# Four graph layers on one core: node numbers kept in SBUF, node phase 2 from centred rows

## The chip, the cores and the metric

One core of a Trainium2 chip runs the kernel. The metric is device time in microseconds, the median of several executions. The profile is of one execution. The engines are TensorE (PE), VectorE (DVE), ScalarE (ACT), GpSimd (POOL) and SyncE (SP), which here only issues and orders DMAs. Operands live in SBUF, with 128 partitions; PSUM takes the results of TensorE.

## The reference

Inputs are x with 64 features per node, src and dst (200,000 edges, dst sorted) and edge attributes. Four layers follow one another, each a residual and a layer norm:

```python
def _layernorm(x): ...                      # over the 64 features
x = _layernorm(x + L0(x, src, dst))         # 4-head attention q.k, gate, norm, PReLU
x = _layernorm(x + L1(x, edge_attr_64))     # graph attention over x[src] + bond, 2 heads
x = _layernorm(x + L2(x, edge_attr_64, ...))# edge attention with messages from [x[src], eh]
x = _layernorm(x + L3(x, edge_attr_32))     # two-layer messages, mean over a node's edges
# L3, for each of its two message layers l:
h = relu(concatenate([x[src], edge_attr]) @ msg_w1[l] + msg_b1[l])
msg += h @ msg_w2[l] + msg_b2[l]
```

Every layer gathers rows by src (one row of a table per edge), computes something per edge, and sums over the edges of each dst, with a running softmax in layers 0 to 2.

## The kernel before

**Layout.** The edges lie in order over the 128 partitions, 1568 per partition (`edges_pp`), 56 chunks of J = 28 edges per partition. Two chunks, b = 0 and b = 1, make a round: 28 rounds for each layer. Nodes lie 98 per partition, in 15 groups for the node phases (up to G = 7 each). A prologue builds tables and masks; then an edge phase and a node phase alternate, k = 0 to 3.

**An edge phase** (class `EdgePhase`) has one program on each engine.

- GpSimd (`gpsimd`, L958 to L984) makes the rows of a chunk: for each of the 28 columns one indirect DMA (L982) gathers 128 table rows, one per partition, by a column of node numbers. Before a chunk it waits for the index tile (`index_in[b]`) and for the chunk's rows to be free (`rows_free[b]`, given by the engine that read the previous contents last). It skips the last column of a chunk b = 1 (`by_sync`) and, every second round, in phases 0, 1 and 3, the one before it (`by_scalar`). The last two columns have semaphores of their own, `last_in` and `other_in`, in the opening rounds in which GpSimd gathers them itself.
- SyncE (`sync`, L781, its `turn`) makes, for each chunk: a wait for each of the seven parts of the gathers of chunk b (so that the index tile may be overwritten), the load of the index tile for the next round (L787, 14 KB), the load of the edge attributes (L791) after `attr_free`, 64 single-row fetches (L871, `fetch`) by numbers that it reads into registers, and, after `ready`, the store of the chunk's sums (L794). Once a round it places the 128 fetched rows as one column of the chunk b = 1 (`place`, L879 to L886). The loop holds two rounds, so that its jump falls between two rounds every second time.
- ScalarE does the exponentials (L1087) and copies, and in phases 0, 1 and 3 fetches 128 rows in two rounds, 32 per chunk (`fetch_rows`, also L871), laid as a column by `lay_rows`.
- VectorE does scans and products. In phase 0 it multiplies k by q (L1355), waits for ScalarE's exponentials, multiplies v by the weights (L1363), which frees the rows, and scans the sums (L1367).
- TensorE works in phases 2 and 3. Phase 2 makes messages and keys for groups of QUAD = 4 columns. Phase 3 multiplies the edge attributes into `e_banks` (L1932, seven 512-wide products for each chunk), which VectorE adds to the gathered hidden rows (L1982); ScalarE applies Relu (L1940), which frees the rows. Semaphore `added` lets TensorE overwrite the banks.

**Node phase 2** (`node_phase_2`, L2581 to L2731) works through the 15 groups in stages written as `in_turn(groups, (delay, stage), ..., per=4)`: on each engine, group g's stage comes at a place that its delay sets. GpSimd gathers the summed rows of the nodes (98 gathers). Aggregation, product with W_out, residual, norm, affine, second norm; then x is scaled by 1 / standard deviation on ScalarE (`finish`, one ACTIVATE per row of 64, L2136), turned and multiplied by the hidden weights on TensorE (L2634); VectorE adds b1 (`take_hidden`, L2718) and SyncE stores the group to `hidden_table`, from which phase 3 gathers. For the first 12 groups a second product of x goes to `aux`. `Norm.turn_over` leaves the reciprocal root in `ph.var`.

Of the kernel before, what the change touches and what calls it, by code (L numbers as in the profile page):

```python
# [29 lines left out]
P = 128  # L30
J = 28
G = 7
# [40 lines left out]
class Program:  # L73


    def __init__(self, nc, ins, out, n_nodes, real_pp, ctx):
# [49 lines left out]
        self.first_src = keep("first_src", [P, 3 * J], U32)  # L126
# [6 lines left out]
        self.skip_gate = keep("skip_gate", [P, self.nodes_pp])  # L133
        self.msg_bias = keep("msg_bias", [P, FD])
# [186 lines left out]
def search_phase(p, sems):  # L321
# [8 lines left out]
    with ExitStack() as ctx:  # L330
# [46 lines left out]
        def _(e):  # L377
# [7 lines left out]
            load(e, p.first_src[:, :], ins["src"][:, 0:3 * J])  # L385
# [44 lines left out]
        def _(e):  # L430
# [9 lines left out]
            for n in range(p.begun):  # L440
                e.indirect_dma_start(p.qv_tiles[n // J][:, n % J, :], None, p.qv_table,
                                     bass.IndirectOffsetOnAxis(ap=p.first_src[:, n:n + 1], axis=0))\
                    .then_inc(p.qv_gathered[n // J][n % J // QUAD], 16)
# [252 lines left out]
class EdgePhase:  # L696


    def __init__(self, p, layer, ctx, gather_from, gather_into, parts=1, gathered=None, merged=False):
# [16 lines left out]
        self.index = [self.sb(f"ix{b}", [P, J], U32) for b in (0, 1)]  # L716
        self.index_in = [self.sem(f"index_in{b}") for b in (0, 1)]
# [63 lines left out]
    def sync(self, e, attrs, size=J):  # L781
# [4 lines left out]
        def load_index(b, now):  # L786
            e.dma_start(self.index[b][:, :], p.ins["src"][:, now]).then_inc(self.index_in[b], 16)  # L787

# [11 lines left out]
        def turn(i, helped=False, helps_next=False, others=None):  # L800
            if helped:
                self.place(e, i, helps_next)
            for b in (0, 1):
                for c in range(self.parts):
                    self.wait_part(e, i, b, c, placed=False)
                if b and self.sync_helps and not helped:
                    self.tell_last(e, i + 1)
                if b and others is not None:
                    hold(e, self.other_in, others, self.passed)
                load_index(b, bass.ds(i * (2 * J) + (2 + b) * J, J))  # L810
# [147 lines left out]
    def gpsimd(self, e):  # L958
# [3 lines left out]
        for i in range(self.rounds):  # L962
            for b in (0, 1):
                n = 2 * i + b
                u = self.buffer(i, b)[0]
                now = self.index[b][:, :] if n >= len(self.gathered) else self.p.first_src[:, n * J:(n + 1) * J]
                if n >= len(self.gathered):
                    e.wait_ge(self.index_in[b], 16 * i)
                    if self.begun and n in (3, 4):
                        e.wait_ge(self.rows_free[1 - b], 2)  # L970
                    else:
                        e.wait_ge(self.rows_free[b], i + 1)
                last = self.p.last if n == self.p.chunks - 1 else J
                for j in range(last):
# [3 lines left out]
                    if J * n + j < done or (last_alone and self.by_sync(i)) or (other_alone and self.by_scalar(i)):  # L978
                        continue
                    landed = self.last_in if last_alone else self.other_in if other_alone else \  # L980
# [13 lines left out]
    def wait_part(self, e, i, b, c, placed=True):  # L994
# [11 lines left out]
        if not self.begun:  # L1006
            e.wait_ge(self.gathered[u][c], at(i, columns - off * b, columns - off * b))
        elif isinstance(i, int) and i < 2:
            e.wait_ge(self.gathered[u][c], (columns, columns - off, columns, 2 * columns - off)[2 * i + b])
        else:  # L1010
            more = columns if b else -off
            if placed:
                e.wait_ge(self.gathered[u][c], at(i, columns - off * b, more))
            else:
                hold(e, self.gathered[u][c - 1], at(i, columns, columns * b), self.passed)
                hold(e, self.gathered[u][c], at(i, columns - off * b, more), self.passed)
        if b and placed and self.sync_helps:
            e.wait_ge(self.placed, at(i, 16, 16))
        if b and placed and self.scalar_step:
# [624 lines left out]
def edge_phase_2(p):  # L1644
# [5 lines left out]
    with ExitStack() as ctx:  # L1650
# [9 lines left out]
        product = ph.sb("product", [P, J, FD])  # L1660
# [149 lines left out]
        def _(e):  # L1810
# [21 lines left out]
            def weigh(i, b, c):  # L1832
# [4 lines left out]
                e.tensor_tensor(product[:, now, :], mk_ps[u][:, :, FD:], q_now[u][:, :, :], ALU.mult)  # L1837
# [3 lines left out]
                e.tensor_reduce(score[:, 0, now], product[:, now, :], AX.X, ALU.add)  # L1841
# [46 lines left out]
def edge_phase_3(p):  # L1888
# [4 lines left out]
    with ExitStack() as ctx:  # L1893
# [32 lines left out]
        def _(e):  # L1926
            with e.Fori(0, ph.rounds) as i:
                for b in (0, 1):
                    ph.wait_attrs(e, i, b, 1)
                    e.wait_ge(added, at(i, 2, b + 1))  # L1930
                    for q in range(quads):
                        last = e.matmul(e_banks[:, q, :], ea_t[b][:, q, :], p.w3_e, start=True, stop=True)  # L1932
# [36 lines left out]
        def _(e):  # L1969
            e.sem_inc(added, 1)  # L1970
            ph.clear_carries(e)
            e.memset(mask[:, :, 0], 0.0)

# [607 lines left out]
def node_phase_2(p):  # L2581
# [3 lines left out]
    with ExitStack() as ctx:  # L2585
# [39 lines left out]
        def _(e):  # L2625
# [3 lines left out]
            def multiply_next(g):  # L2629
# [12 lines left out]
                else:  # L2642
# [5 lines left out]
                    (17, turn_next),  # L2648
                    (19, multiply_next), per=4)

        @block.scalar
        def _(e):
# [4 lines left out]
            def finish(g):  # L2657
                second.act_scale(e, g, p.x[:, ph.now(g), :]).then_inc(times_next.given, 1)

            def take_next(g):  # L2660
                if g < early:
# [9 lines left out]
                    (12, lambda g: second.act_square(e, g, p.x[:, ph.now(g), :])),  # L2671
                    (14, lambda g: second.act_root(e, g, p.eps[:, 0:1])),
                    (16, finish),
                    (18, lambda g: times_next.move(e, g)),
                    (20, take_next), per=4)

        @block.vector
        def _(e):
# [34 lines left out]

            def take_hidden(g):
                n = ph.sizes[g]
                after(e, stored[g % outs], 16 * (g // outs))
                e.wait_ge(made, g + 1)
                e.tensor_tensor(hidden_out[g % outs][:, 0:n, :],  # L2718
                                hidden_ps.rearrange("p k (u f) -> p (k u) f", u=2)[:, 0:n, :],
                                bcast(p.param["L3_gnn_msg_b1"][:, :], 1, n), ALU.add)  # L2720
                e.drain().then_inc(taken, 1)
# [8 lines left out]
                    (15, lambda g: second.turn_over(e, g)),  # L2730
                    (20, take_hidden), per=4)  # L2731
# [223 lines left out]
```

## Time and profile before

| | |
|---|---|
| median of 3 runs | 14026.2 us (14020.19 to 14042.77) |
| profiled execution | 14023.7 us, its span 14022.0 us |
| mean granted TensorE clock | 0.575 |
| POOL busy | 6487.0 us, 46% |
| DVE busy | 4894.6 us, 35% |
| ACT busy | 3146.0 us, 22% |
| PE busy | 2267.2 us, 16% |

Busy time leaves out DMA issues and register work, so SyncE has no share, and ScalarE's fetches are not in its 22%. A group's second part is the idle time of its engine before it, with what ended most of it. In a timeline, consecutive like instructions are one row: start, time from the first to the end of the last, and their count.

### The profile page before, as it was taken

How to read it: one execution, taken by the hardware profiler on the slowest of the kernel's cores; microseconds unless marked ns; L12 is line 12 of the kernel's file. 1: busy time of each engine (PE TensorE's matmuls, PEld its weight loads, DVE VectorE, ACT ScalarE, POOL GpSimd, SP SyncE). 2: the span in 40 equal slices, each digit the busy share in tenths (PEclk: the TensorE clock that was granted, in tenths of full speed). 3: DMA queues.
4: the chain of work that ended last, by engine and by line, in shares of the span. 5: the costliest groups of instructions: out<-in, count | busy, mean ns of one | idle time of the engine just before them, and what ended most of it. 6: DMA issues, size and time to landing. Idle time of an engine off the chain costs nothing. (4 is left out here: it accounts for less than half of the span.)

```text
span 14022.0 us, 92846 instructions
## 1 busy us (share of the span) xinstructions
PE 2267.2 (16%) x11897; PEld 1811.0 (13%) x11897; DVE 4894.6 (35%) x6191; ACT 3146.0 (22%) x3841; POOL 6487.0 (46%) x6837
## 2 busy tenths in 40 slices
PE   2000000002000000000344433444432111111112
PEld 1000000001000000000244333433330000000002
DVE  3443333345444444445222222222242222222223
ACT  0221111114111111112132222332232222222222
POOL 6644444456544444444544444444434444444444
PEclk6555555555555555555677777777765555555556
DMA  6222222221222222222222222222212222222222
GB/s 239 81 73 70 74 70 74 70 90 34 63 66 65 65 70 68 65 65 81 61 79 78 71 77 80 79 79 71 77 44 68 70 67 72 72 72 72 71 71 69
DMA packets 418910, 1046.03 MB, mean 75 GB/s; under 512 B 198760, under 2 KB 226218, under 8 KB 403804
## 3 DMA queue, kind: packets, MB, share of 16 engines
q1 hardware_dynamic: 177424, 680.51, 13.0%
q0 software_dynamic: 219488, 334.23, 10.0%
q10 hardware_dynamic: 21612, 27.96, 0.6%
q14 instruction: 366, 3.00, 0.1%
q8 instruction: 20, 0.33, 0.0%
HBM read 633.14 MB, written 401.95 MB: 74 GB/s over the span
## 5 line engine op out<-in xcount | busy, mean ns | idle before, releaser
L982 POOL DMA_INDIRECT se<-x_table,edge_ix x1481 | 1400.8, 946 | 1855.7 <-DMA edge_ix<-in_src 815.7
L982 POOL DMA_INDIRECT hidden<-hidden_table,edge_ix x1468 | 1388.7, 946 | 1761.0 <-DMA edge_ix<-in_src 1289.8
L982 POOL DMA_INDIRECT g<-x_table,edge_ix x1468 | 1388.5, 946 | 1648.8 <-DMA edge_ix<-in_src 1169.1
L982 POOL DMA_INDIRECT qv<-qv_table,edge_ix x1443 | 1378.6, 955 | 1404.4 <-DMA edge_ix<-in_src 865.8
L1144 ACT ACTIVATE edge_sums<-edge_val 128x1904 f32<-128x1904 f32 (+3 forms) x220 | 1116.4, 5075 | 1084.9 <-issue 1050.9
L1837 DVE TENSOR_TENSOR edge_product<-mk_ps,edge_q_now 128x256 f32<-128x256 f32 x391 | 166.1, 425 | 2308.8 <-ACT edge_msg L1772 2262.0
L1134 DVE TENSOR_TENSOR_SCAN edge_val<-edge_bank,edge_val 128x464 f32<-128x464 f32 (+1 forms) x715 | 687.6, 1032 | 672.0 <-ACT edge_val L1940 441.6
L1932 PE MATMUL edge_e_ps<-w_nodes,edge_ea_t 128*128 128x512 f32 x784 | 476.6, 774 | 2733.9 <-DMA edge_ea_t<-in_edge_attr 1165.2
L1982 DVE TENSOR_TENSOR hidden<-hidden,edge_e_ps 128x3584 f32<-128x3584 f32 x55 | 213.8, 3888 | 1799.2 <-DMA hidden<-edge_sync_rows 1232.4
L1727 PE MATMUL mk_ps<-w_mk,edge_se_t 128*128 128x128 f32 x3128 | 523.1, 320 | 1656.6 <-issue 1399.5
L1087 ACT ACTIVATE edge_bank<-edge_weight_arg 128x112 f32<-128x112 f32 (+2 forms) x171 | 38.9, 228 | 2939.9 <-issue 1980.9
L1727 PEld LDWEIGHTS mk_ps<-w_mk,edge_se_t 128*128 128x128 f32 x3128 | 459.0, 225 | 1712.4 <-issue 1419.2
L1355 DVE TENSOR_TENSOR edge_product<-edge_k_ps,qv 128x896 f32<-128x896 f32 x110 | 182.4, 1658 | 1413.4 <-DMA qv<-edge_sync_rows 900.4
L1940 ACT ACTIVATE edge_val<-hidden 128x3584 f32<-128x3584 f32 x55 | 346.4, 6298 | 1430.5 <-DVEq L1983 845.1
L1522 DVE TENSOR_TENSOR g<-g,edge_bond_ps 128x1792 f32<-128x1792 f32 (+2 forms) x56 | 111.3, 1988 | 1463.0 <-DMA g<-edge_sync_rows 1126.2
L1932 PEld LDWEIGHTS edge_e_ps<-w_nodes,edge_ea_t 128*128 128x128 f32 x784 | 192.3, 254 | 3017.8 <-issue 1926.2
L1271 PE MATMUL edge_bond_ps<-ident,edge_fix_wide 128*128 128x128 f32 x4 | 1.2, 461 | 3157.8 <-DVEq L1231 3157.8
L1271 PE MATMUL edge_k_ps<-ident,edge_fix_wide 128*128 128x128 f32 x8 | 2.1, 441 | 2982.5 <-DVEq L1231 2982.5
L1143 ACT ACTIVATE edge_sums<-edge_peak 128x112 f32<-128x112 f32 (+2 forms) x165 | 50.3, 305 | 1849.5 <-issue 1791.2
L1134 DVE TENSOR_TENSOR_SCAN edge_val<-edge_decay,edge_val 128x464 f32<-128x464 f32 (+1 forms) x440 | 459.0, 1117 | 6.6
L1762 ACT ACTIVATE edge_se_t<-se_ps 128x512 f32<-128x512 f32 x391 | 234.0, 598 | 932.0 <-DMA node_first_er<-er_table,first_index 556.7
L1770 ACT ACTIVATE edge_q_now<-qo_ps 128x256 f32<-128x256 f32 x391 | 150.7, 385 | 1287.4 <-DMA edge_ix<-in_src 762.4
(463 smaller groups left out, 8657.6 us busy)
## 6 DMA issues: line engine op xcount, KB each, us to landing
edge_sync_rows<-x_table SPq DMA_DIRECT2D x6656, 0.2 KB
sums<-edge_sums SPq DMA_DIRECT2D x55, 1848.0 KB
sums<-edge_sums SPq DMA_DIRECT2D x55, 1792.0 KB
sums<-edge_sums SPq DMA_DIRECT2D x55, 1008.0 KB
edge_sync_rows<-hidden_table SPq DMA_DIRECT2D x3328, 0.5 KB
sums<-edge_sums SPq DMA_DIRECT2D x55, 924.0 KB
edge_k<-k_edges SPq DMA_DIRECT2D x56, 896.0 KB
edge_bond<-in_edge_attr SPq DMA_DIRECT2D x56, 896.0 KB
```

Of the source, the lines that this page charges most:

```text
L982: e.indirect_dma_start(self.gather_into(u, j), None, self.gather_from, bass.IndirectOffsetOnAxis(ap=now[:, j:j + 1], axis=0))\
L1134: return e.tensor_tensor_scan(out=now, data0=keep[:, 0:n, :].rearrange("p f j -> p (f j)"), data1=now, initial=0.0, op0=ALU.mult, op1=ALU.add)
L1144: e.activation(self.sums[b][:, :, 0:n], self.val[b][:, :, 1:].rearrange("p f j -> p j f"), ACT.Copy)\
L1355: e.tensor_tensor(product[:, 32 * half:32 * half + 32, :], k_ps[:, :, 1:], q[:, 32 * half:32 * half + 32, :], ALU.mult)
L1522: e.tensor_tensor(g[b][:, now, :], g[b][:, now, :], bond_ps[:, now, :], ALU.add)
L1727: e.matmul(mk_ps[u][:, j, :], se_t[u][:, j, :], p.w2_mk[:, :], start=True, stop=True)
L1762: e.activation(se_t[u][:, :, :], se_ps[u][:, :, :], ACT.Copy)
L1770: e.activation(q_now[u][:, :, :], qo_ps[:, :, :].rearrange("p a (c f) -> p (a c) f", c=2), ACT.Copy)
L1837: e.tensor_tensor(product[:, now, :], mk_ps[u][:, :, FD:], q_now[u][:, :, :], ALU.mult)
L1932: last = e.matmul(e_banks[:, q, :], ea_t[b][:, q, :], p.w3_e, start=True, stop=True)
L1940: e.activation(ph.val[b][:, :, 1:], g[b].rearrange("p j f -> p f j"), ACT.Relu).then_inc(taken, 1)
L1982: e.tensor_tensor(g[b][:, :, :], g[b][:, :, :], e_ps, ALU.add)
```

## The change

The node numbers (`src`, 802 KB) are loaded whole into a tile `p.src` in the prologue. The index tiles, their loads and semaphores, and SyncE's waits on the gathered parts go. GpSimd waits only for `rows_free`, and in the opening rounds for `placed` and `laid` ahead of the last two columns. In phase 2 the product tile becomes two tiles of QUAD columns. Node phase 2 multiplies the centred, unscaled x: ScalarE takes each row of the product with its factor (`scale=` of ACTIVATE) and stages come earlier. The factors are kept in `x_scale`, with which VectorE scales x and aux at the start of phase 3. b1 is added in phase 3 by a second product on TensorE, ones x b1, into the same bank.

```diff
-        self.first_src = keep("first_src", [P, 3 * J], U32)
+        self.src = keep("src_now", [P, self.edges_pp], U32)
...
+        self.x_scale = keep("x_scale", [P, self.nodes_pp])
...
-            load(e, p.first_src[:, :], ins["src"][:, 0:3 * J])
+            load(e, p.src[:, :], ins["src"][:, :])
...
-                for c in range(self.parts):
-                    self.wait_part(e, i, b, c, placed=False)
                 if b and self.sync_helps and not helped:
                     self.tell_last(e, i + 1)
-                if b and others is not None:
-                    hold(e, self.other_in, others, self.passed)
-                load_index(b, bass.ds(i * (2 * J) + (2 + b) * J, J))
                 hold(e, self.attr_free[b], at(i, 1, 1), self.passed)
...
-                now = self.index[b][:, :] if n >= len(self.gathered) else self.p.first_src[:, n * J:(n + 1) * J]
+                now = self.p.src[:, n * J:(n + 1) * J]
                 if n >= len(self.gathered):
-                    e.wait_ge(self.index_in[b], 16 * i)
...
+                    if last_alone and i:
+                        e.wait_ge(self.placed, 16 * i)
+                    if other_alone and i:
+                        e.wait_ge(self.laid, 16 * i)
...
-        product = ph.sb("product", [P, J, FD])
+        product = [ph.sb(f"product{u}", [P, QUAD, FD]) for u in (0, 1)]
...
-                        last = e.matmul(e_banks[:, q, :], ea_t[b][:, q, :], p.w3_e, start=True, stop=True)
+                        e.matmul(e_banks[:, q, :], ea_t[b][:, q, :], p.w3_e, start=True, stop=False)
+                        last = e.matmul(e_banks[:, q, :].rearrange("p (c f) -> p c f", c=QUAD), p.ones[0:1, :],
+                                        bcast(p.param["L3_gnn_msg_b1"][0:1, :], 1, QUAD), start=False, stop=True)
...
-            e.sem_inc(added, 1)
             ph.clear_carries(e)
             e.memset(mask[:, :, 0], 0.0)
+            scale, scaled = e_banks[:, 0, 0:p.nodes_pp], p.nodes_pp - sum(ENDS) - (LATE - len(ENDS)) * G
+            e.tensor_copy(scale, p.x_scale[:, :])
+            e.drain()
+            e.tensor_tensor(p.x[:, :, :], p.x[:, :, :], bcast(scale, 2, FD), ALU.mult)
+            e.tensor_tensor(p.aux[:, 0:scaled, :], p.aux[:, 0:scaled, :], bcast(scale[:, 0:scaled], 2, FD), ALU.mult)
+            e.drain().then_inc(added, 1)
...
-                    (17, turn_next),
-                    (19, multiply_next), per=4)
+                    (12, turn_next),
+                    (14, multiply_next), per=4)
...
-            def finish(g):
-                second.act_scale(e, g, p.x[:, ph.now(g), :]).then_inc(times_next.given, 1)
+            def take_hidden(g):
+                after(e, stored[g % outs], 16 * (g // outs))
+                e.wait_ge(made, g + 1)
+                e.wait_ge(second.turned_over, g + 1)
+                rows = hidden_ps.rearrange("p k (u f) -> p (k u) f", u=2)
+                for t in range(ph.sizes[g]):
+                    at_ = ph.first[g] + t
+                    e.activation(hidden_out[g % outs][:, t, :], rows[:, t, :], ACT.Copy, scale=ph.var[:, at_:at_ + 1])
+                e.drain().then_inc(taken, 1)
...
+                    (13, lambda g: times_next.move(e, g)),
                     (14, lambda g: second.act_root(e, g, p.eps[:, 0:1])),
-                    (16, finish),
-                    (18, lambda g: times_next.move(e, g)),
-                    (20, take_next), per=4)
+                    (15, take_next),
+                    (16, take_hidden), per=4)
...
-            def take_hidden(g):
-                n = ph.sizes[g]
-                after(e, stored[g % outs], 16 * (g // outs))
-                e.wait_ge(made, g + 1)
-                e.tensor_tensor(hidden_out[g % outs][:, 0:n, :],
-                                hidden_ps.rearrange("p k (u f) -> p (k u) f", u=2)[:, 0:n, :],
-                                bcast(p.param["L3_gnn_msg_b1"][:, :], 1, n), ALU.add)
-                e.drain().then_inc(taken, 1)
+                e.sem_inc(times_next.given, 1)
...
+            e.tensor_copy(p.x_scale[:, :], ph.var[:, :])
```

## Rows read from the trace of the kernel before

**Rows 1.** The page, busy us (share of the span) xinstructions of each engine.

```profile
PE 2267.2 (16%) x11897; PEld 1811.0 (13%) x11897; DVE 4894.6 (35%) x6191; ACT 3146.0 (22%) x3841; POOL 6487.0 (46%) x6837
```

**Rows 2.** The page's costliest groups, the gathers: phases 2, 3, 1, 0.

```profile
L982 POOL DMA_INDIRECT se<-x_table,edge_ix x1481 | 1400.8, 946 | 1855.7 <-DMA edge_ix<-in_src 815.7
L982 POOL DMA_INDIRECT hidden<-hidden_table,edge_ix x1468 | 1388.7, 946 | 1761.0 <-DMA edge_ix<-in_src 1289.8
L982 POOL DMA_INDIRECT g<-x_table,edge_ix x1468 | 1388.5, 946 | 1648.8 <-DMA edge_ix<-in_src 1169.1
L982 POOL DMA_INDIRECT qv<-qv_table,edge_ix x1443 | 1378.6, 955 | 1404.4 <-DMA edge_ix<-in_src 865.8
```

**Rows 3.** Timeline, SyncE, phase 0: start us, us, engine line, xcount.

```profile
2006.75 0.40 SPq L794 DMA_DIRECT2D sums<-edge_sums  x1
2007.99 0.37 SPq L787 DMA_DIRECT2D edge_ix<-in_src  x1
2008.63 0.94 SPq L791 DMA_DIRECT2D edge_k<-k_edges  x1
2011.85 45.24 SPq L871 DMA_DIRECT2D edge_sync_rows<-qv_table  x64
2057.36 0.39 SPq L794 DMA_DIRECT2D sums<-edge_sums  x1
...
2058.63 0.96 SPq L886 DMA_DIRECT2D qv<-edge_sync_rows  x1
...
2063.86 47.86 SPq L871 DMA_DIRECT2D edge_sync_rows<-qv_table  x64
...
2113.06 0.37 SPq L787 DMA_DIRECT2D edge_ix<-in_src  x1
```

**Rows 4.** Timeline, SyncE, phase 1, over the loop's jump.

```profile
5307.87 0.39 SPq L794 DMA_DIRECT2D sums<-edge_sums  x1
...
5314.66 0.50 SPq L886 DMA_DIRECT2D g<-edge_sync_rows  x1
```

**Rows 5.** Timeline, fetches by window: 2020:2043, 2047:2057.2, 3560:3626 (SyncE), 3520:3640 (ScalarE).

```profile
2020.96 20.47 SPq L871 DMA_DIRECT2D edge_sync_rows<-qv_table  x11
...
2046.33 10.76 SPq L871 DMA_DIRECT2D edge_sync_rows<-qv_table  x30
...
3565.86 59.00 SPq L871 DMA_DIRECT2D edge_sync_rows<-x_table  x22
...
3575.73 64.03 ACTq L871 DMA_DIRECT2D edge_scalar_rows<-x_table  x32
```

**Rows 6.** Timeline, VectorE, ScalarE, GpSimd, phase 0: [idle before <-releaser].

```profile
2073.02 3.22 DVE L1363 TENSOR_TENSOR edge_val<-qv,edge_bank 128x1792 f32<-128x1792 f32 x1 [0.33 <-issue]
...
2086.87 21.17 ACTq L871 DMA_DIRECT2D edge_scalar_rows<-qv_table  x32
2109.79 0.27 ACT L1087 ACTIVATE edge_bank<-edge_weight_arg 128x112 f32<-128x112 f32 x1 [25.24 <-DVE edge_decay_arg L1078]
...
2116.35 0.95 POOL L982 DMA_INDIRECT qv<-qv_table,edge_ix  x1 [19.32 <-DMA edge_ix<-in_src]
```

**Rows 7.** Timeline, GpSimd and ScalarE, phase 2.

```profile
8546.83 0.94 POOL L982 DMA_INDIRECT se<-x_table,edge_ix  x1 [27.69 <-PEq L1717]
...
8586.47 0.38 ACT L1770 ACTIVATE edge_q_now<-qo_ps 128x256 f32<-128x256 f32 x1 [13.75 <-DMA edge_ix<-in_src]
...
8606.53 0.95 POOL L982 DMA_INDIRECT se<-x_table,edge_ix  x1 [24.97 <-DMA edge_ix<-in_src]
```

**Rows 8.** Groups of instructions in 10283 to 10550, node phase 2.

```profile
L2136 ACT ACTIVATE x_now<-x_now,node_var 128x64 f32<-128x64 f32 x98 | 24.9, 336 | 0.4 <-DVEq L2126 0.3
...
L2718 DVE TENSOR_TENSOR node_hidden_out<-node_hidden_ps,bc_L_gnn_msg_b 128x896 f32<-128x896 f32 (+2 forms) x15 | 15.3, 1021 | 18.5 <-DMA sums<-edge_fix_row,fix_to 15.1 <-PE node_hidden_ps L2634 3.4
```

**Rows 9.** Windows, node phase 2: window, us, busy us (xcount) of each engine, clock, DMA share, GB/s.

```profile
10450.00:10500.00 50.00, 32.77 (x157) 26.73 (x156) 42.72 (x85) 34.46 (x110) 0.00 (x0) 0.83 0.12 47
```

**Rows 10.** The page's costliest groups, TensorE in phase 3.

```profile
L1932 PE MATMUL edge_e_ps<-w_nodes,edge_ea_t 128*128 128x512 f32 x784 | 476.6, 774 | 2733.9 <-DMA edge_ea_t<-in_edge_attr 1165.2
```

More of the change, by code:

```diff
@@ L441, in _ @@
                 e.indirect_dma_start(p.qv_tiles[n // J][:, n % J, :], None, p.qv_table,
-                                     bass.IndirectOffsetOnAxis(ap=p.first_src[:, n:n + 1], axis=0))\
+                                     bass.IndirectOffsetOnAxis(ap=p.src[:, n:n + 1], axis=0))\
                     .then_inc(p.qv_gathered[n // J][n % J // QUAD], 16)
@@ L715, in __init__ @@
         self.sums = [self.sb(f"sums{b}", [P, J, self.width]) for b in (0, 1)]
-        self.index = [self.sb(f"ix{b}", [P, J], U32) for b in (0, 1)]
-        self.index_in = [self.sem(f"index_in{b}") for b in (0, 1)]
         self.attr_in = [self.sem(f"attr_in{b}") for b in (0, 1)]
@@ L784, in sync @@
         out = p.sums[self.k].rearrange("(p j) f -> p j f", p=P)
-        def load_index(b, now):
-            e.dma_start(self.index[b][:, :], p.ins["src"][:, now]).then_inc(self.index_in[b], 16)
         def load(b, n):
@@ L992, in buffer, with wait_part @@
         return 1 - b, (i, 1, b)
-    def wait_part(self, e, i, b, c, placed=True):
+    def wait_part(self, e, i, b, c):
         u, (times, per, more) = self.buffer(i, b)
@@ L1010, in wait_part @@
         else:
[L1011 to L1017, printed above, removed]
+            e.wait_ge(self.gathered[u][c], at(i, columns - off * b, columns if b else -off))
+        if b and self.sync_helps:
             e.wait_ge(self.placed, at(i, 16, 16))
-        if b and placed and self.scalar_step:
+        if b and self.scalar_step:
             e.wait_ge(self.laid, at(i, 16, 16))
@@ L1836, in weigh @@
                 now = slice(QUAD * c, QUAD * (c + 1))
-                e.tensor_tensor(product[:, now, :], mk_ps[u][:, :, FD:], q_now[u][:, :, :], ALU.mult)
+                e.tensor_tensor(product[u][:, :, :], mk_ps[u][:, :, FD:], q_now[u][:, :, :], ALU.mult)
                 e.scalar_tensor_tensor(msg[:, now, :], mk_ps[u][:, :, 0:FD], 0.01, msg[:, now, :],
@@ L1840, in weigh @@
                 e.drain()
-                e.tensor_reduce(score[:, 0, now], product[:, now, :], AX.X, ALU.add)
+                e.tensor_reduce(score[:, 0, now], product[u][:, :, :], AX.X, ALU.add)
             def chunk(i, b):
@@ L2729, in _ @@
                     (13, lambda g: second.sum_squares(e, g)),
-                    (15, lambda g: second.turn_over(e, g)),
-                    (20, take_hidden), per=4)
+                    (15, lambda g: second.turn_over(e, g)), per=4)
+            e.tensor_copy(p.x_scale[:, :], ph.var[:, :])
 def node_phase_3(p):
```

## The prediction

> **What bounds the kernel now.** I read the shares of busy time first [rows 1]: no engine is full; GpSimd at 46% is the fullest, and TensorE's granted clock plays no part since TensorE has 16%. So the bound is an order of waits, and the costliest groups say where [rows 2]. The indirect gathers of the four edge phases (L982) run at one per 1.25 us (0.95 busy, 0.30 before it), and after each chunk's burst GpSimd stands still; most of that is put down to the index tile's load, 815.7 + 1289.8 + 1169.1 + 865.8 = 4140 us. At some 54.5 gathers a round (28 + 26 or 27; 55 in phase 2) busy and idle give the period of a round: phase 0 (1378.6 + 1404.4)/26.5 = 105 us, phase 1 113, phase 2 121, phase 3 117.
>
> "Waits for the index" isn't "the index is dear". SyncE's queue row by row [rows 3] shows a queue that never rests: store, index load, attribute load, 64 row fetches, store, placing of the fetched column, index, attributes, 64 fetches. The index load is one instruction in that chain and comes late because the fetches ahead of it are late. A round there takes 2113.06 - 2007.99 = 105.1 us, of which the fetches are 45.2 + 47.9 = 93.1 and everything else 12.0. Every second round the loop's jump lies between the store and the placing, 5314.66 - 5307.87 = 6.8 us instead of 2058.63 - 2057.36 = 1.3 [rows 4], on average 2.7 more.
>
> Why do 64 fetches take 45 us? By [rows 5], between bursts 30 take 10.76 us, 0.36 each; within a burst 11 take 20.47 us, 1.9 each on average over a window that begins before they slow. Of the 64, that leaves 23 for the first 9 us, from 2011.85 to 2020.96, so the start of a burst is quick too. In the long opening burst of phase 1, 22 take 59.00 us: 2.7 each; 32 of ScalarE's take 64.03. So a burst of GpSimd's gathers slows SyncE's fetches some eightfold after a quick start, until about 3 to 5 us after the last gather. The round is therefore: two bursts, in which 33 or so fetches each get through, and gaps in which the rest (some 62) and the 12.0 + 2.7 us of other instructions are done. SyncE paces phases 0, 1 and 3; VectorE and ScalarE wait for its column.
>
> [...]
>
> **Part 1: the index stays in SBUF.** Removed on SyncE: per chunk a load (issue to next row 0.64 us, [rows 3]) and, ahead of it, the waits for the seven parts of the gathers and, every second round, for `other_in`. Store to attribute load is 2008.63 - 2006.75 = 1.88 us, of which the store 0.40; the removed part lies between 0.64 and 1.5 us, and I take 1.1 per chunk. On the path for sure is only one of a round's two, since the other lies ahead of the hold on `placed`, whose DMA is in flight anyway. Floor: 1.1 us a round.
>
> The larger effect is that GpSimd no longer waits for SyncE's order. A burst now starts when `rows_free` allows. Take placing at 2058.63 as 0. The second chunk's rows are freed by the multiply L1363, 2073.02 + 3.22 = 2076.2, so at +17.6 [rows 6]; that chunk's next burst started at 2116.35, +57.7, after 19.3 us of rest. Now they will run: second chunk's burst from +17.6 to +51 (27 x 1.25 = 33.8). ScalarE's 32 fetches begin at +28.2 (2086.87), inside that burst, so at 2.7 us until +55: 10 of them; 22 more at 0.36 take it to +63; then the exponentials that now come at 2109.79, and L1363, 3.5 us further: +66.6. That frees the first chunk's rows, and its burst runs +66.6 to +101.6. So ScalarE, not SyncE, releases every second burst; the gap before it is 15.6 us, where the gaps were 19 to 20.
>
> SyncE's 128 fetches then decide the placing. From +4.2 to +17.6 it does 37, in the next 9 us the rest of 64; its store, loads and register work (5.2 us, or 4.1 without the index) now fall under the burst, where they cost slow time, worth 2 or 3 fetches, instead of gap. The other 64: some 7 until +55, 30 in the gap to +66.6, 23 in the burst's first 9 us, 4 left, which are slow: placing near +87 or, if the quick start is a few fetches shorter, past +100. A placing that comes early is followed by a late one (both bursts then touch, and one quick start is lost), so I take the budget: of the 14.7 us that lay in gaps, 1.1 to 2.2 vanish and about a third, 4.9 us, goes under a burst at the price of 3 fetches, 1.1 us. That is 1.1 + 4.9 - 1.1 = 4.9, say 5 us a round in phase 0 (ends: 1.1, and 1.1 + 14.7 - 2 = 13.8). In phases 1 and 3 ScalarE's fetches stand ahead of more of its own work and the rounds are longer for the same SyncE chain; there I take 3.5 and 2.5. With 24 rounds in each that follow the loop: 24 x (5 + 3.5 + 2.5) = 264 us.
>
> Phase 2: ScalarE does not fetch there, but its chain with TensorE makes no progress inside a burst either: in the burst from 8546.83 (28 gathers, 35 us) it stands idle for 13.75 us until 8586.47, five microseconds after the last gather [rows 7]. The rows come free only 20 us after the burst; the burst at 8546.83 was released by TensorE, that at 8606.53 by the index, which landed just behind. Estimate 0.9 us in 32 of 56 chunks: 30 us (ends 0 and 56 x 2.7).
>
> GpSimd's new waits on `placed` and `laid` lie in the opening rounds alone, where those columns are its own gathers and long signalled: 0, at most 3 phases x 2 rounds x 5 us = 30. The whole list (802 KB for 43 KB) loads in the prologue on SyncE's queue beside the clearing of tables: 0 to +5 us, I take +2.
>
> **Part 2: halves of the product tile in phase 2.** Same instructions, same sizes: 0.
>
> **Part 3: node phase 2.** VectorE loses L2718, 15 x 1021 ns = 15.3 us; ScalarE loses the 98 scalings of x (336 ns each, 24.9 us [rows 8]) and gains 98 ACTIVATEs of 128 elements. From 64 elements at 336 ns I bound one between 336 and 672 ns and take 390: 38 us. In the stretch after the gathers VectorE is busy 42.72 of 50 us, ScalarE 34.46 [rows 8, 9]; 13 more over 15 groups is 0.9 us a group. A group takes about 10 us there, so ScalarE goes from 6.9 to 7.8 of each 10, still under VectorE's 8.5. VectorE bounds this stretch, where 11 or more of the 15 groups run: 11 x 1.1 = -12 us; four more run beside GpSimd's gathers at no gain. The shorter stage list brings the end 2 stages nearer: 2 us. Sum -14 (ends 0, should the wait for the ScalarE results replace the add, and -25; if one ACTIVATE took 672 ns, ScalarE at 9.1 of 10 us would pass VectorE and the part would cost +5). The Trainium skill's "ScalarE: Activation LUTs" gives a fixed cost and a price per element by which one would take roughly 350 to 390 ns, as an estimate; with it the part would come out the same.
>
> **Part 4: phase 3.** The multiplies of x and aux by x_scale at the start: 11,648 elements per partition; L1363 takes 1792 in 3.22 us, so at most 21 us. They run while GpSimd makes its first burst (28 x 1.25 = 35 us) before any chunk can be added: 0, up to +10 if they are slowed or the Block begins with a late GpSimd. b1 on TensorE: as many more matmuls as L1932 has (784 records, 476.6 us busy, 8.5 us a chunk, [rows 10]); TensorE idles 2733.9 us before them and e_ps is wanted one chunk (59 us) later. But it can start only once the previous add has read the banks and, in a burst, at stretched pace: 0, up to +1 us a chunk in 28 of the chunks.
>
> **Sum.** The profiled run took 14023.7 us (span 14022.0), 2.5 below the median of 14026.2. -264 - 30 + 2 - 14 = -306 on the median: 13,720.
>
> **Rivals.** (a) *Only the instructions count.* The fetches fill SyncE's chain as before and the starts fall such that nothing is covered: 1.1 x 75 + 0 to 30 + 14 = 96 to 126, so about 13,910. For it: SyncE has no rest in [rows 3], and in-burst time is worth little. Against: 14.7 us a round plainly lie in GpSimd's gaps. (b) *Slower: bursts merge.* If the first chunk's burst follows the second's directly, there is one burst of 67 us. SyncE loses one quick start (20 fetches done at 0.4 instead of slow: 20 x 0.36 = 7.2 us that must be made up in a gap) and saves one recovery (3 to 5 us); ScalarE's own fetches are slow throughout, 32 take 64 us as in the opening burst of phase 1 [rows 5], and its sums come late. Net +2 to +4 us a round over 75: +150 to +300, less 44 for parts 3 and phase 2 when those hold: 14,130 to 14,250, take 14,170. It decides once ScalarE's fetches are done before the burst ends; against it is that they begin inside it. (c) *Everything goes under cover*: 9 to 12 us a round in phase 0 and 1 and 6 in phase 3, 24 x 27 = 650: 13,330. For it: the first chunk's placing can come as early as +87. [...]
>
> **Chances.** Forecast 0.45, (a) 0.21, (b) 0.19, (c) 0.13, (d) 0.02. Range 13,400 to 14,130, which leaves out the far parts of (b) and (c). About 0.2% (28 us) is what a measurement of this kernel can tell from no change. Slower by more: 0.17 from (b); within: 0.02 from each of (a), (b) and the forecast's edge, 0.07; faster 0.76.
>
> **What would show it.** SyncE's rows without index loads, store to attribute load under 1 us. GpSimd's idle before L982 released by ScalarE, VectorE or `rows_free`, with the second chunk's burst some 18 us after the placing in phase 0. Fetches in bursts still at 2.7 us. Bursts of phase 0 that alternate gaps of about 15 and 20 us. Node phase 2's tail after the last node gather shorter by 14 us. It is wrong if bursts touch round after round, or if the rounds lose only 1 us.

## The result and the profile after

| | median of runs | profiled span |
|---|---|---|
| before | 14026.1 us (14020.19 to 14042.77) | 14022.0 us |
| changed | 14249.86 us (14245.8 to 14255.44) | 14247.4 us |

The ratio is 1.0158, 95% interval 1.014 to 1.0175: the change costs 224 us, where the forecast was 306 us less.

On the changed kernel's page, four groups of gathers (their line is L976 now) are the counterpart of [rows 2]; they count phase 0's and the other phases' opening gathers too, which had a name of their own before:

```profile
L976 POOL DMA_INDIRECT hidden<-hidden_table,src_now x1524 | 1441.1, 946 | 1951.4 <-ACTq L1932 1370.4
L976 POOL DMA_INDIRECT se<-x_table,src_now x1537 | 1453.2, 945 | 1843.9 <-PEq L1706 1387.2
L976 POOL DMA_INDIRECT g<-x_table,src_now x1524 | 1441.1, 946 | 1703.3 <-DVEq L1538 1245.3
L976 POOL DMA_INDIRECT qv<-qv_table,src_now x1485 | 1418.0, 955 | 1566.7 <-DVEq L1353 1125.0
```

The index has gone as a releaser, and the idle time has not shrunk. What releases a burst now is whoever frees the rows: VectorE in phases 0 and 1, ScalarE in phase 3, TensorE in phase 2.

From placing to placing, the trace gives these mean rounds (first to last placing of each phase, over the number of rounds between; e11 is the changed kernel with a token added, told of under the experiments):

| phase | before | changed | e11 (token) |
|---|---|---|---|
| 0 | 107.3 us | 114.6 | 104.5 |
| 1 | 113.8 | 115.8 | 107.7 |
| 2 | 120.7 | 119.5 | 119.4 |
| 3 | 118.4 | 120.9 | 111.1 |

Times the rounds (23, and three times 25) that is +170, +51, -30 and +63 us. The stretches between the phases give back 17.5, 7.5 and 8.4 us, the prologue 1.3, and the tail behind the last placing takes 6.3 more: +225 in all, which is the difference of the two profiled spans.

SyncE's queue over one round of phase 0 in the changed kernel, the counterpart of [rows 3] (start us, us, xcount):

```profile
2035.49 0.50 SPq L877 DMA_DIRECT2D qv<-edge_sync_rows  x1
2036.29 0.37 SPq L787 DMA_DIRECT2D edge_k<-k_edges  x1
2039.67 49.59 SPq L862 DMA_DIRECT2D edge_sync_rows<-qv_table  x64
2089.53 0.39 SPq L790 DMA_DIRECT2D sums<-edge_sums  x1
2090.20 0.36 SPq L787 DMA_DIRECT2D edge_k<-k_edges  x1
2094.91 51.21 SPq L862 DMA_DIRECT2D edge_sync_rows<-qv_table  x64
2146.38 0.39 SPq L790 DMA_DIRECT2D sums<-edge_sums  x1
2147.84 0.23 SPq L868 DMA_DIRECT2D edge_at_sync<-row_at  x1
2148.19 0.92 SPq L877 DMA_DIRECT2D qv<-edge_sync_rows  x1
```

The index loads are gone, and the instructions that aren't fetches still take 112.7 - 100.8 = 11.9 us, as before (12.0): from the store to the load of the attributes it is 0.67 us instead of 1.88, but from there to the first fetch 4.71 instead of 3.22. The fetches take 49.6 + 51.2 = 100.8 us instead of 93.1. GpSimd's bursts in the same round, with what released them:

```profile
2052.35 0.95 POOL L976 DMA_INDIRECT qv<-qv_table,src_now  x1 [33.18 <-DVEq L1353]
...
2103.27 0.95 POOL L976 DMA_INDIRECT qv<-qv_table,src_now  x1 [18.70 <-DVEq L1353]
...
2165.70 0.94 POOL L976 DMA_INDIRECT qv<-qv_table,src_now  x1 [27.71 <-DVEq L1353]
```

They start 16.9 and 67.8 us after the placing at 2035.49, where +17.6 and +66.6 were forecast. Only the next placing isn't where it was put: it comes at +112.7.

### The profile page after: what moved, and what is told of

Read it like the earlier page. It is cut to its first block and busy times, and to the rows that moved or that the text cites. A ratio compares the mean times of both kernels' runs of the same rounds, so it can differ in the third digit from the quotient of the medians.

```text
span 14247.4 us, 92537 instructions
## 1 busy us (share of the span) xinstructions
PE 3362.0 (24%) x12681; PEld 2012.2 (14%) x12681; DVE 4893.6 (34%) x6180; ACT 3143.3 (22%) x3841; POOL 6482.0 (45%) x6837
## 5 line engine op out<-in xcount | busy, mean ns | idle before, releaser
L976 POOL DMA_INDIRECT hidden<-hidden_table,src_now x1524 | 1441.1, 946 | 1951.4 <-ACTq L1932 1370.4
L976 POOL DMA_INDIRECT se<-x_table,src_now x1537 | 1453.2, 945 | 1843.9 <-PEq L1706 1387.2
L976 POOL DMA_INDIRECT g<-x_table,src_now x1524 | 1441.1, 946 | 1703.3 <-DVEq L1538 1245.3
L976 POOL DMA_INDIRECT qv<-qv_table,src_now x1485 | 1418.0, 955 | 1566.7 <-DVEq L1353 1125.0
L1921 PE MATMUL edge_e_ps<-w_nodes,edge_ea_t 128*128 128x512 f32 x784 | 813.6, 1141 | 1717.3 <-DVEq L1979 975.2
L1922 PE MATMUL edge_e_ps<-bc_L_gnn_msg_b,ones 1*128 1x512 f32 x784 | 811.8, 1136 | 0.0
L1536 DVE TENSOR_TENSOR edge_val<-g,edge_bank 128x1792 f32<-128x1792 f32 x110 | 345.2, 3179 | 375.8 <-ACT edge_bank L1076 290.3
```

What stands on the lines that cost most here:

```text
L976: e.indirect_dma_start(self.gather_into(u, j), None, self.gather_from, bass.IndirectOffsetOnAxis(ap=now[:, j:j + 1], axis=0))\
L1536: e.tensor_tensor(ph.values(b)[:, n, :, :], rows_now, bcast(ph.weight[:, n, :], 1, FD), ALU.mult)
L1922: last = e.matmul(e_banks[:, q, :].rearrange("p (c f) -> p c f", c=QUAD), p.ones[0:1, :], bcast(p.param["L3_gnn_msg_b1"][0:1, :], 1, QUAD) ...
```

## The experiments

Each kernel ran beside the kernel before on the same chip, and the chips differ. On the chip of the first comparison, on e5's and on that of e11 and e12, the kernel before takes 13,945 to 14,027 us. On the chips of all other runs it takes 8788 to 8802 us. What sets them apart is told under e1 to e4. Only e5, e11 and e12 can tell of the 224 us.

**e5, the changed kernel again**, no edit.

> The changed kernel as it stands, beside the kernel before on the same chip, where the earlier comparison had 14,250 against 14,026 us. If SyncE's and ScalarE's fetches are slowed within GpSimd's bursts, 14,230 to 14,270 us beside 14,026. If they are not (as in the four runs above, where the kernel before took 8788 us), GpSimd's gathers are back to back, and the order of starts has nothing to give or to lose: 8,775 to 8,795 us, node phase 2 and phase 3 deciding.

Measured: 14180.86 us against 13944.9, ratio 1.0171 (1.0154 to 1.0188). The loss is there in a second comparison of this kind. The trace has the same pattern: bursts at +17.2 and +66.0 us after the placing in phase 0, a round of 112.5 us.

**e1 to e4.** e1 is the changed kernel with a token: SyncE increments a semaphore where it loaded the index tile, and GpSimd waits for it.

```diff
+TURNS = {0: (0, 1), 1: (0, 1), 3: (0, 1)}
 # SyncE, in turn(), before the hold on attr_free
+                if b in TURNS.get(self.k, ()):
+                    e.sem_inc(self.turned[b], 1)
 # GpSimd, ahead of the wait for rows_free
+                    if b in TURNS.get(self.k, ()):
+                        e.wait_ge(self.turned[b], i)
```

> The changed kernel, in which SyncE gives a token (a semaphore increment, no DMA) where it loaded the index tile, and GpSimd waits for it before each burst in phases 0, 1 and 3; phase 2 stays free. Theory S (order): the loss of some 7 us a round in phase 0 comes from bursts that start as soon as rows are free; with the token, rounds go back to about 107, 114 and 118 us, phase 2 keeps its gain of 30 us, so 13,970 to 14,010 us. Rival R (SyncE's own pace without the index loads and part waits makes it slower, whatever GpSimd does): 14,200 or more. Rival N (the node phase 2 and b1 part is what costs): within 40 us of the changed kernel.

e2 is the kernel before with the hunks of parts 1 and 2 (`p.src`, SyncE's waits, the product tile); e3 the kernel before with the hunks of node phase 2 and phase 3.

> The kernel before with the node numbers in SBUF and the product tile halved, node phase 2 and phase 3 as before. Theory S: the whole loss is here, 14,240 to 14,270 us. Rival N: about 14,000 us.

> The kernel before with the changes of node phase 2 and phase 3 alone. Theory S: between 9 us less (node phase 2) and 10 us more (b1 in phase 3's tail), so 14,017 to 14,040 us. Rival N: 14,150 or more.

e4 is the changed kernel without b1's product, so that b1 is missing from its result:

```diff
-                        e.matmul(e_banks[:, q, :], ea_t[b][:, q, :], p.w3_e, start=True, stop=False)
-                        last = e.matmul(e_banks[:, q, :].rearrange("p (c f) -> p c f", c=QUAD), p.ones[0:1, :],
-                                        bcast(p.param["L3_gnn_msg_b1"][0:1, :], 1, QUAD), start=False, stop=True)
+                        last = e.matmul(e_banks[:, q, :], ea_t[b][:, q, :], p.w3_e, start=True, stop=True)
```

> The changed kernel without the second product on TensorE: b1 is left out of the result. In the trace VectorE waits 243 us for that product (L1922), in 19 waits. If ScalarE's fetches end later anyway (theory S), the time falls by 0 to 15 us, most of it in phase 3's tail. If TensorE is on the path in phase 3, it falls by 50 to 200 us.

Measured, against 8787.92 us: e1 8786.6 (0.9998, 0.9989 to 1.0008), e2 8793.57 (1.0004, 0.9995 to 1.0014), e3 8783.81 (0.9996, 0.9987 to 1.0006), e4 8778.5 (0.9989, 0.998 to 0.9999). No expectation of a time in us was met, since all of them took a kernel of 14,000 us for granted. The reason stands in the queue of SyncE; the kernel of e1 on another chip of this kind (run e6), phase 0:

```profile
1339.90 0.50 SPq L881 DMA_DIRECT2D qv<-edge_sync_rows  x1
1340.79 0.37 SPq L789 DMA_DIRECT2D edge_k<-k_edges  x1
1344.58 23.26 SPq L866 DMA_DIRECT2D edge_sync_rows<-qv_table  x64
...
1374.63 23.08 SPq L866 DMA_DIRECT2D edge_sync_rows<-qv_table  x64
...
1408.89 0.97 SPq L881 DMA_DIRECT2D qv<-edge_sync_rows  x1
```

and its gathers on the page:

```profile
L982 POOL DMA_INDIRECT hidden<-hidden_table,src_now x1524 | 1438.1, 944 | 506.4 <-issue 506.1
L982 POOL DMA_INDIRECT qv<-qv_table,src_now x1485 | 1401.7, 944 | 453.0 <-issue 447.8
```

Here 64 fetches take 23 us, 0.36 us each, with GpSimd gathering all the while. GpSimd waits for nobody: its idle time is the 0.30 us between gathers. The round is 68.2 us, which is 54.5 x 1.25, so GpSimd alone sets the time, and which engine frees what and when is nothing to it. A gather takes the same on both kinds of chip (0.95 + 0.30 us). What differs is that on the slower kind SyncE's fetches drop to some 2 to 3 us each inside a burst.

**e6 to e9**, e1's kernel again, two kernels with one of the two tokens (`TURNS = {0: (0,), 1: (0,), 3: (0,)}` and `(1,)`), and e3's again.

> The kernel of e1 once more, since e1's chip does not slow the fetches in bursts. Where the kernel before takes some 14,000 us, theory S (order): phases 0, 1 and 3 back at about 107, 114 and 118 us a round, and 33, 31 and 26 of SyncE's fetches in each burst as before (the changed kernel has 29, 22 and 21): 10 to 60 us below the kernel before. Rival R (SyncE without its index loads and waits is slower by itself): 150 us or more above it. Where the kernel before takes 8788 us: same, as in e1.

> The token for the bursts of the first chunk alone: they wait until SyncE has placed its column, those of the second start when rows are free. The placing and the second chunk's rows lie 15 to 25 us apart, so the second burst follows the first with no gap: one burst of 67 us, one quick start. Theory S with the count of quick starts as what matters: 20 fetches fewer in bursts, +2 to +8 us a round, 150 to 500 us above the kernel before. If only the state of SyncE at a burst's start matters (rested or in the middle of fetching), near the kernel before, within 60 us. Where the kernel before takes 8788 us: same.

> The token for the bursts of the second chunk alone: they wait until SyncE's first 64 fetches are done, those of the first chunk start when ScalarE's exponentials have freed their rows. Theory S: the second chunk's burst starts with SyncE rested (34 fetches in it), the first's at any time: between turns_back and the changed kernel, 0 to 150 us above the kernel before. Where the kernel before takes 8788 us: same.

> The kernel of e3 once more. Where the kernel before takes some 14,000 us: node phase 2 shorter by 8 to 10 us, phase 3's tail longer by some 6, and VectorE's waits for the second product (243 us in all) behind other waits: within 20 us of the kernel before. Rival N: 100 us or more above it, in phase 3. Where it takes 8788 us: same, as in e3.

Measured against 8790.65 us: 8787.38, 8785.52, 8787.73 and 8784.15, ratios 0.9997, 0.9997, 0.9997 and 0.9995, every interval with 1 in it. The chip doesn't slow the fetches, so they are the same, as was expected for such a chip; the question wasn't answered. Nor was it by e10 (e1's kernel) and by e13 and e14 (those of e7 and e8):

> The kernel of e1 and e6 a third time. Where the kernel before takes some 14,000 us: theory S, 10 to 60 us below it, with 33, 31 and 26 fetches of SyncE in a burst of phases 0, 1 and 3; rival R, 150 us or more above it. Where it takes 8788 us: same.

> The kernel of e7, for a chip that slows the fetches in bursts. The token for the bursts of the first chunk alone. If both bursts must keep their place in SyncE's order, it lies between the kernel with both tokens (13,585 us) and the changed kernel (14,250): the second chunk's burst starts on rows free, 17 to 25 us after the placing, while the first is still running, so it follows at once: one burst of 67 us, one quick start instead of two, 13,900 to 14,300 us. If only the first chunk's burst matters: 13,550 to 13,650.

> The kernel of e8, for a chip that slows the fetches in bursts. The token for the bursts of the second chunk alone. Theory S: the first chunk's rows come free some 20 us after the second burst's end, before the placing, so the first burst starts 10 to 20 us earlier than with both tokens and takes the quick time of the last fetches ahead of the placing: 13,700 to 14,100 us. If only the second chunk's burst matters: 13,550 to 13,650.

Measured: e10 8798.13 against 8801.95 us, e13 and e14 8787.99 and 8786.7 against 8788.83, all same.

**e11 and e12**, the kernels of e1 and e3 on a chip that slows the fetches.

> The kernel of e1 for a chip that slows the fetches in bursts. There: theory S, 10 to 60 us below the kernel before (about 14,000 us), with 33, 31 and 26 fetches of SyncE in a burst of phases 0, 1 and 3; rival R, 150 us or more above it. On a chip where the kernel before takes some 8790 us: same.

> The kernel of e3 for a chip that slows the fetches in bursts. There: within 20 us of the kernel before (node phase 2 shorter by 8 to 10 us, phase 3's tail longer by some 6); rival N, 100 us or more above it. On a chip where the kernel before takes some 8790 us: same.

Measured against 14027.21 us: e12 14019.21 (0.9994, 0.9982 to 1.0005), e11 **13584.62 us** (0.9684, 0.9656 to 0.9712). e12 clears node phase 2 and b1: rival N is out, and the loss is in part 1 (the halves of the product tile are in the changed kernel and in e11 alike). e11's time is of two executions, 13580.67 and 13588.58. e11 has all of part 1 except that GpSimd may not run ahead of SyncE, and it is 443 us faster than the kernel before, where the changed kernel is 1.6 to 1.7% slower. Rival R, that SyncE without its loads is slow by itself, is out. Theory S had the sign and not the size (10 to 60 us expected), and its count of fetches was missed as well: 33, 31 and 26 in a burst of phases 0, 1 and 3 were expected, and on average 29.7, 28.1 and 23.2 get through. Its SyncE and GpSimd in phase 0:

```profile
2016.20 0.96 SPq L881 DMA_DIRECT2D qv<-edge_sync_rows  x1
2017.56 0.36 SPq L789 DMA_DIRECT2D edge_k<-k_edges  x1
2021.72 44.02 SPq L866 DMA_DIRECT2D edge_sync_rows<-qv_table  x64
2066.00 0.39 SPq L792 DMA_DIRECT2D sums<-edge_sums  x1
2066.75 0.36 SPq L789 DMA_DIRECT2D edge_k<-k_edges  x1
2071.32 42.40 SPq L866 DMA_DIRECT2D edge_sync_rows<-qv_table  x64
...
2119.88 0.50 SPq L881 DMA_DIRECT2D qv<-edge_sync_rows  x1
```

```profile
2017.48 0.94 POOL L982 DMA_INDIRECT qv<-qv_table,src_now  x1 [18.46 <-SPq L805]
...
2066.72 0.94 POOL L982 DMA_INDIRECT qv<-qv_table,src_now  x1 [14.58 <-SPq L805]
```

A burst starts 1.3 us after the placing and 0.7 us after the store. In the kernel before it was 2062.31 - 2058.63 = 3.7 and, by [rows 6], 2116.35 - 2111.97 = 4.4:

```profile
2062.31 0.94 POOL L982 DMA_INDIRECT qv<-qv_table,edge_ix  x1 [18.97 <-DMA edge_ix<-in_src]
...
2111.97 0.40 SPq L794 DMA_DIRECT2D sums<-edge_sums  x1
```

That is 6.1 us a round in which the bursts come earlier; the rounds are shorter by 2.8, 6.1 and 7.3 us in phases 0, 1 and 3. Beside e12, which ran on the same chip (rounds of 107.0, 113.6 and 118.5 us), it is 2.5, 5.9 and 7.4.

**e15 to e18: how early, and is it the landing?** e15 and e17 give each token in the middle of the 64 fetches before; e16 and e18 are e11's kernel with the index load back behind the token, unread and not waited for by GpSimd.

```diff
 # e15, e17
-                    self.fetch(e, slice(b * P // 2, (b + 1) * P // 2), self.at_sync, self.sync_rows, self.sync_in)
+                    first = b * P // 2
+                    self.fetch(e, slice(first, first + BATCH), self.at_sync, self.sync_rows, self.sync_in)
+                    if self.k in TURNS:
+                        e.sem_inc(self.turned[1 - b], 1)
+                    self.fetch(e, slice(first + BATCH, first + P // 2), self.at_sync, self.sync_rows, self.sync_in)
 # e16, e18
                     e.sem_inc(self.turned[b], 1)
+                    hold(e, self.index_in[b], at(i, 16, 0), self.passed)
+                    e.dma_start(self.index[b][:, :], p.ins["src"][:, bass.ds(i * (2 * J) + (2 + b) * J, J)])\
+                        .then_inc(self.index_in[b], 16)
```

> Both tokens, each given in the middle of the 64 fetches before (after 32) instead of after them and the store. 'Earlier is better' (each burst 2.5 us earlier in SyncE's order was worth 2.5 us from the kernel before to e11): 32 x 0.36 = 11 us earlier twice a round, 13,000 to 13,400 us. Theory S (a burst that starts while SyncE still has fetches to do slows them, and the placing with them): 13,800 to 14,400 us.

> The kernel of e11, with the index load back on SyncE behind the token, into a tile that nobody reads; GpSimd doesn't wait for it. It tells the price of the instruction from that of its landing. If what e11 won is the landing (GpSimd's start at +1 us instead of +3.5), 13,590 to 13,670 us. If it is the instruction itself, 13,900 us or more.

> The kernel of e15 for a chip that slows the fetches in bursts. Both tokens in the middle of the 64 fetches before. 'Earlier is better': 13,000 to 13,400 us. Theory S: 13,800 to 14,400 us. Where the kernel before takes some 8790 us: same.

> The kernel of e16 for a chip that slows the fetches in bursts. If what e11 won is the landing of the index tile, 13,590 to 13,670 us; if it is the instruction on SyncE itself, 13,900 us or more. Where the kernel before takes some 8790 us: same.

Both came twice onto chips that don't slow the fetches: e15 8786.89 and e16 8786.31 against 8788.83, e17 8785.9 and e18 8785.09 against 8790.4, all same. Neither question is settled where it matters.

## Why the prediction was wrong

**What was right.** The mechanism at work (GpSimd's bursts slow SyncE's and ScalarE's fetches, after a quick start) carries all of it, and on the chips where it is absent nothing of the change can be measured. So were the bursts' new starts, +16.9 and +67.8 for +17.6 and +66.6, and ScalarE as what holds the second back: the multiply of VectorE that frees its rows waits for ScalarE's exponentials.

```profile
2099.75 3.22 DVE L1352 TENSOR_TENSOR edge_val<-qv,edge_bank 128x1792 f32<-128x1792 f32 x1 [28.78 <-ACT edge_bank L1076]
```

Phase 2 gained 30 us as forecast. In node phase 2 one of the new ACTIVATEs takes 389 ns (390 forecast):

```profile
L2660 ACT ACTIVATE node_hidden_out<-node_hidden_ps,node_var 128x128 f32<-128x128 f32 x98 | 27.0, 389 | 3.0 <-PE node_hidden_ps L2630 2.9
```

and GpSimd's rest behind the node gathers fell by 9 us (14 forecast), from 141.59 us before to 132.49:

```profile
10548.04 0.95 POOL L982 DMA_INDIRECT hidden<-hidden_table,first_src  x1 [141.59 <-issue]
...
10702.31 0.94 POOL L976 DMA_INDIRECT hidden<-hidden_table,src_now  x1 [132.49 <-issue]
```

**The step that failed** is the one on SyncE's fetches: "From +4.2 to +17.6 it does 37, in the next 9 us the rest of 64", and from it "placing near +87" and the budget in which "about a third, 4.9 us, goes under a burst at the price of 3 fetches". On it rest the -264 us of phases 0, 1 and 3 in the sum, where the rounds took 284 us more. SyncE's rows in the changed kernel, in the windows 2039:2051, 2051:2058.5 and 2058.5:2089.5, which hold the first 64 fetches, and in 2052.3:2084.6 and 2103.2:2138, a whole burst each:

```profile
2039.67 10.71 SPq L862 DMA_DIRECT2D edge_sync_rows<-qv_table  x32
...
2052.66 5.67 SPq L862 DMA_DIRECT2D edge_sync_rows<-qv_table  x16
...
2058.77 30.50 SPq L862 DMA_DIRECT2D edge_sync_rows<-qv_table  x16
...
2052.66 30.09 SPq L862 DMA_DIRECT2D edge_sync_rows<-qv_table  x28
...
2103.22 35.47 SPq L862 DMA_DIRECT2D edge_sync_rows<-qv_table  x27
```

At the start of the burst 32 were done, not 37; the next 32 numbers were just being read into registers. The quick start let 16 more through in 6 us (2052.35 to 2058.3), where 27 in 9 us had been put. So 16 of the first 64 were left, and they took 30.5 us, nearly the whole burst. They ended at 2089.3, +53.8, instead of +27. The second 64 began at 2094.91, behind the store and the load, only 8.4 us before the second burst, and ran into it in the same way: 27 of them fell into the burst, and the last into the time behind it. The placing waited until that burst was over, and since the second chunk's rows come free only 17 us after a placing, GpSimd rested 27.71 us. The chain of a round has become placing, 17 us, burst, ScalarE's fetches and exponentials (2062.71 to 2099.7), burst, SyncE's last slow fetches, placing. Before, a burst lay over the first 35 us of it.

The quick start also isn't a property of the burst alone, as I had taken it: "the start of a burst is quick too". Counted over the trace (18 to 20 rounds of each phase, SyncE's fetches from the first gather of a burst to its last):

| | phase 0, two bursts | phase 1 | phase 3 | fetches in the 5 us before a burst, phase 0 |
|---|---|---|---|---|
| before | 31.9 + 34.5 | 32.2 + 29.6 | 28.1 + 24.1 | 0, 1 |
| changed | 29.4 + 28.2 | 20.2 + 23.1 | 20.0 + 21.6 | 9, 14 |
| e11 | 28.2 + 31.2 | 30.6 + 25.6 | 27.0 + 19.4 | 3, 12 |

In the kernel before, a burst met SyncE at its store and its loads, with fetches yet to begin. In the changed kernel it meets SyncE in the middle of fetching, and 9, 19 and 11 fetches a round fewer get through. That the one makes the other is not shown: e11's second burst has 12 fetches in the 5 us before it and lets 31 through, more than its first with 3 and 28, and e15 on a chip of that kind is missing. And it isn't the larger part: e11 gets hardly more fetches through in phase 0 (59.4 against 57.6), and its round is 10 us shorter.

The larger part is where SyncE's other instructions lie. GpSimd's two gaps of a round in phase 0 add up to 39.5 us before, 46.9 changed and 36.7 in e11 (means over 18 rounds). The changed kernel's 46.9 can be estimated: 128 - 57.6 = 70.4 fetches at 0.36 are 25 us, twice 5 us until fetches are quick again after a burst, and 12 us of store, loads, placing and reading of numbers, all of which lie in gaps (2089.53 to 2094.91, 2146.38 to the first fetch at 2153.03), since both bursts start in the middle of a block of fetches. That is 47, and with the 2.7 us of the loop's jump, which it leaves out, 50. The same working, the jump counted, gives about 45 for the kernel before and 41 for e11: 3 to 5 us too high each time, with the differences between the three kernels right to 2 us. In e11 a burst starts as such a stretch begins, and 2021.72 - 2017.48 = 4.2 and 2071.32 - 2066.72 = 4.6 us of it run within the quick start. That is the saving I had put into the budget for the changed kernel, where it could not be: it needs the order that the change took away.

**The rivals.** (b) had the sign, and 14,170 us. Its mechanism was not the one, so the nearness of its 14,170 to the measured 14,250 is luck: in phase 0 the bursts don't merge (gaps of 16.5 and 30.4 us on average). In phase 1 they nearly do (8.8 and 39.1), and there the loss is only 2 us a round. My argument against (b), that ScalarE's fetches begin inside the burst and so keep the bursts apart, held in phase 0 and did not save it. I had asked what makes bursts start earlier, and not what keeps a fetch block from straddling one. (a)'s floor was not a floor: it took the order for fixed. A case in which bursts slow nothing, (d) with its 0.02 in the chances, is what four other chips show: the fetches run at 0.36 us through every burst. There GpSimd is the bound at 68 us a round, but it is so for the kernel before as well, and the change gains nothing.

**The second product in phase 3** is dearer than put down: TensorE's granted clock is 0.50 there (10700:13000), its level of 1.2 GHz, where it was 0.56 before, and 811.8 us in 56 chunks make 14.5 us a chunk, where 8.5 were forecast; the first product slowed from 8.5 to 14.5 us with it (476.6 to 813.6 us in all, [rows 10]). In places VectorE waits for it (phase 3, VectorE and ScalarE):

```profile
12036.73 3.89 DVE L1978 TENSOR_TENSOR hidden<-hidden,edge_e_ps 128x3584 f32<-128x3584 f32 x1 [12.73 <-PE edge_e_ps L1922]
...
12054.58 6.24 ACT L1931 ACTIVATE edge_val<-hidden 128x3584 f32<-128x3584 f32 x1 [24.73 <-issue]
```

but ScalarE, whose fetches last until 12054.47, takes the rows up only then. e12, with this product and without part 1, is within 0.2% of the kernel before. Where GpSimd sets the time, e4, which leaves it out, is 8 us below e1 and 9 below the kernel before, at the edge of what can be told.

**What stays open.** Why some chips slow the fetches: the kernel and the gathers are the same, and so are the transfers (a packet of the queue that holds SyncE's loads and fetches takes 165 ns on average in e12 and 166 in e9, the same kernel). No chip is known to have been seen as both kinds, so whether the chip makes the difference or something that ran beside it isn't shown. How the 443 us of e11 divide between the index tile's landing, its instruction and SyncE's waits for parts; which of the two tokens is needed; whether a still earlier token would pay. The best version where fetches are slowed is e11's, 3.2% below the kernel before; elsewhere all versions lie within 0.15% of it.

## What to carry to other kernels

A wait that looks like pure latency can be the pacing of two engines: before it goes, follow the engine that gets slowed, instruction by instruction, through the new starts, and see whether its block ends before the slow time or just inside it. If it doesn't, keep the order and drop only the latency: a semaphore in the place of the transfer won here what removing the wait lost twice over. And run both kernels on more than one chip before believing in the bound.

## What the runs showed of the hardware

The same kernel takes some 8790 us on four chips and some 14,000 us in the other three comparisons, e5, e11 with e12, and the first. There, a fetch of SyncE or ScalarE takes 1.9 to 2.7 us (16 in 30.50, 22 in 59.00) instead of 0.36 once a burst of GpSimd's indirect DMAs has run for some 4 to 11 us (averages of phases 0, 1 and 3 in the kernel before, the changed one and e11; 6 in the burst at 2052.35), and until some 4 to 5 us after it. GpSimd's own gathers take 0.95 + 0.30 us on either kind.

It is not only the instruction that issues the DMA. Between two fetches stands a MOVE, which sets a register and issues nothing, and it is slowed as much (count, ns min/median/max; the changed kernel in 2040:2050, before the burst, and in 2059:2089, within it, then e6 in 1344:1368, where GpSimd gathers too):

```profile
L862 SPq MOVE edge_sync_rows<-qv_table x30: 29/29/37, 2040.0 to 2049.8; - x30
...
L862 ACTq MOVE edge_scalar_rows<-qv_table x16: 29/690/709, 2062.7 to 2086.9; - x16
...
L862 SPq MOVE edge_sync_rows<-qv_table x14: 3/699/712, 2059.5 to 2088.3; - x14
...
L866 SPq MOVE edge_sync_rows<-qv_table x64: 29/29/42, 1344.5 to 1367.6; - x64
```

So what a burst slows on these chips is the flow of instructions of SyncE and ScalarE, with or without a DMA; the transfers take no longer than on the other kind (165 and 166 ns a packet, above). GpSimd's own MOVEs take at most 35 ns in the trace of the kernel before, SyncE's up to 1457. Why it is so, the runs don't show.
